# Expert gating with its counts ahead of its ranks, and one wait of the key-shared attention placed behind a projection

## The reference

```python
probs = jax.nn.softmax(x @ gate_w, axis=-1)
w, sel = jax.lax.top_k(probs, K)                    # K = 8 of E = 32
w = w / jnp.sum(w, axis=-1, keepdims=True)
flat_e = sel.reshape(-1)
order = jnp.argsort(flat_e)
se = flat_e[order]
start = jnp.searchsorted(se, jnp.arange(E))
pos = jnp.arange(P) - start[se]
slot = jnp.where(pos < C, se * C + pos, E * C)      # C = 2 * (P // E)
```

```python
gating = jax.nn.softmax(x @ W_gate.T, axis=-1)
idx = jnp.argmax(gating, axis=-1)
indicator = jax.nn.one_hot(idx, H, dtype=gating.dtype)
gating_top1 = indicator * jnp.max(gating, axis=-1, keepdims=True)
q, k, v = jnp.split(x @ W_qkv.T, 3, axis=-1)
k_shared = jnp.einsum('bth,bthd->btd', indicator, k)
v_shared = jnp.einsum('bth,bthd->btd', gating_top1, v)
att = softmax(causal(einsum('bhqd,bkd->bhqk', q, k_shared) / sqrt(hd)))
y = jnp.einsum('bhqk,bkd->bhqd', att, v_shared)
```

## Time and profile before

| what | value |
|---|---|
| median of three runs | 2397.06 us |
| profiled execution, its own time | 2396.05 us |
| its span | 2394.0 us |
| PE busy | 2161.7 us (90%) |
| PEld busy | 1379.3 us (58%) |
| DVE busy | 1525.1 us (64%) |
| ACT busy | 1116.3 us (47%) |
| POOL busy | 741.6 us (31%) |
| mean granted TensorE clock | 0.958 |

### The profile page before, as it was taken

One profiled execution on the slowest core, in us unless ns is written; L12 is line 12 of the kernel. 1 busy time (PEld: TensorE's weight loads), 2 busy tenths in 40 slices (PEclk: granted clock), 3 DMA queues, 4 the chain that ended last, 5 costly groups with the idle time before them and its releaser, 6 DMA issues. The chain is left out here.

```text
span 2394.0 us, 38433 instructions
## 1 busy us (share of the span) xinstructions
PE 2161.7 (90%) x10486; PEld 1379.3 (58%) x10486; DVE 1525.1 (64%) x3718; ACT 1116.3 (47%) x3541; POOL 741.6 (31%) x930
## 2 busy tenths in 40 slices
PE   6978999989799799979999999999998698879999
PEld 3445677766555344445565666566665455545675
DVE  6975434446566577755577777777777688842234
ACT  2021234421355355545555655565554488822342
POOL 5715510046233200013344444444443200003104
PEclk9968999999999899989999999999999699969999
DMA  6902245544400000000000000000000000201243
GB/s 214 312 29 77 91 125 161 164 153 115 170 1 0 3 1 0 0 27 1 1 1 1 0 1 0 1 1 0 1 0 1 5 6 5 109 3 52 68 130 100
DMA packets 85614, 127.41 MB, mean 53 GB/s; under 512 B 12418, under 2 KB 74626, under 8 KB 84226
## 3 DMA queue, kind: packets, MB, share of 16 engines
q1 hardware_dynamic: 75490, 98.52, 12.8%
q0 software_dynamic: 9984, 27.28, 3.6%
HBM read 91.41 MB, written 47.84 MB: 58 GB/s over the span
## 5 line engine op out<-in xcount | busy, mean ns | idle before, releaser
L2442 ACT ACTIVATE l2x_prob<-l2x_pS,l2x_nb,l2x_rms_q 128x256 f32<-128x256 f32 x256 | 142.5, 565 | 147.1 <-DVE l2x_nb L2691 145.3
L1035 ACT ACTIVATE moe_act_g<-moe_pG 128x96 f32<-128x96 f32 (+1 forms) x159 | 53.4, 336 | 266.2 <-PE moe_pU L968 185.8
L1199 PE MATMUL l2x_pQ<-big,l2x_xT 128*128 128x512 f32 x312 | 149.6, 602 | 4.8 <-DVE l2x_part L2669 4.3
L3212 DVE TENSOR_TENSOR l3f_hid<-l3f_act_g,l3f_pA 128x256 f32<-128x256 f32 (+1 forms) x103 | 38.1, 370 | 163.3 <-ACT l3f_act_g L3123 119.5
L928 POOL DMA_INDIRECT moe_yk<-route_y,moe_slot_i x72 | 71.4, 992 | 216.2 <-DMA route_y<-moe_y 187.6
L2240 PE MATMUL l2x_pOT<-l2x_probT,l2x_v 128*128 128x512 f32 x256 | 126.4, 616 | 12.3 <-ACT l2x_probT L2457 12.3
L2230 PE MATMUL l2x_pS<-l2x_kT,l2x_qT 128*128 128x256 f32 x512 | 129.8, 383 | 0.0
L3036 PE MATMUL l3f_pA<-big,l3f_xnT 128*128 128x512 f32 x256 | 126.1, 617 | 0.0
L2247 PE MATMUL l2x_pT<-big,l2x_oT 128*128 128x256 f32 x512 | 123.8, 379 | 0.0
L3123 ACT ACTIVATE l3f_act_g<-l3f_pA 128x256 f32<-128x256 f32 (+1 forms) x103 | 35.4, 344 | 184.6 <-PE l3f_pA L3036 184.6
L2688 DVE TENSOR_REDUCE l2x_negmax<-l2x_pS 128x2 f32<-128x512 f32 x128 | 87.5, 684 | 52.3 <-PE l2x_pS L2230 50.6
(11 more groups left out here) (538 smaller groups left out, 5735.8 us busy)
## 6 DMA issues: line engine op xcount, KB each, us to landing
route_x<-in_c_zero SPq DMA_DIRECT2D x1, 13184.0 KB, 80.5
moe_xg<-route_x SPq DMA_DIRECT2D x103, 128.0 KB, 2.1
route_y<-moe_y SPq DMA_DIRECT2D x103, 128.0 KB, 1.7
big<-in_e_gu SPq DMA_DIRECT2D x1, 6144.0 KB, 18.9
l3f_xg<-route_x SPq DMA_DIRECT2D x39, 128.0 KB, 2.2
route_y<-l3f_y SPq DMA_DIRECT2D x39, 128.0 KB, 1.7
big<-in_f_gu SPq DMA_DIRECT2D x1, 4096.0 KB, 12.5
big<-in_e_down SPq DMA_DIRECT2D x1, 3072.0 KB, 25.6
```

What stands on the lines that cost most here:

```text
L1199: last = pe.matmul(out, lhsT=xT[:, k, :], rhs=w[:, k, cols], start=(k == 0), stop=(k == KC - 1))
L2442: ins = act.activation(prob[g % 2][:, h, :], pS[j][:, (h % 2) * 2 * P:(h % 2 + 1) * 2 * P], ACT.Exp, scale=rms_q[g][:, h:h + 1], bias=nb[: ...
```

## The change

In gating the nine matmuls of the counts go ahead of those of the ranks and raise a semaphore of their own, `counts`. VectorE rounds the counts behind that one. The triangle `below`, its load and the product with it are gone; the offsets come from a running sum over the 32 experts in five rounds, each a copy of the first columns and an addition of the rest shifted by 1, 2, 4, 8 or 16. `until` is the scaled sum and `offs` that minus the expert's own count. The weights are normalised next, and only then does VectorE wait for `ranks` and make the slots. In the key-shared attention the wait for `normalised` moves from ahead of the value projection to behind it, ahead of the projection into `pQK`.

```diff
@@ -696,10 +696,10 @@
         replaced, top = ph.sb("replaced", [P, B, NE]), ph.sb("top", [P, B, 8])
         chosen, probs = ph.sb("chosen", [P, B, NE], BF16), ph.sb("probs", [P, B, NE])
         red, rec = ph.sb("red", [P, B]), ph.sb("rec", [P, B])
-        lower, onesb, below = ph.sb("lower", [P, P], BF16), ph.sb("onesb", [P, P], BF16), ph.sb("below", [P, NE * NE])
-        prod = ph.sb("prod", [P, NE, NE])
-        const_in, xT_ps, xT_ready, logits, steps, masks, ranks, exp_done = (
-            ph.sem(n) for n in ("const_in", "xT_ps", "xT_ready", "logits", "steps", "masks", "ranks", "exp_done"))
+        lower, onesb = ph.sb("lower", [P, P], BF16), ph.sb("onesb", [P, P], BF16)
+        sums = [ph.sb(f"sums{i}", [P, NE]) for i in range(2)]
+        const_in, xT_ps, xT_ready, logits, steps, masks, counts, ranks, exp_done = (
+            ph.sem(n) for n in ("const_in", "xT_ps", "xT_ready", "logits", "steps", "masks", "counts", "ranks", "exp_done"))
         need, offs, until, slot = G["need"], G["offs"], G["until"], G["slot"]
         block = ph.block()
 
@@ -720,7 +720,6 @@
         def _(sp):
             sp.dma_start(lower[:].bitcast(U16), D["c_lower"]).then_inc(const_in, 16)
             sp.dma_start(onesb[:].bitcast(U16), D["c_onesb"]).then_inc(const_in, 16)
-            sp.dma_start(below[:], D["c_below32"].partition_broadcast(P)).then_inc(const_in, 16)
 
         @block.tensor
         def _(pe):
@@ -747,15 +746,16 @@
                 turn(b)
                 scores(b - 1)
             scores(B - 1)
-            pe.wait_ge(const_in, 48)
+            pe.wait_ge(const_in, 32)
             pe.wait_ge(masks, 1)
             picked = chosen[:].rearrange("p b e -> p (b e)")
+            for b in range(SB):
+                last = pe.matmul(pC[:, 0:NE], lhsT=onesb[:], rhs=chosen[:, b, :], start=(b == 0), stop=(b == SB - 1))
+            last.then_inc(counts, 1)
             pe.matmul(pR[:], lhsT=lower[:], rhs=picked, start=True, stop=True)
             for d in range(1, B):
-                pe.matmul(pR[:, d * NE:], lhsT=onesb[:], rhs=picked[:, 0:(B - d) * NE], start=False, stop=True,
-                          skip_group_check=True)
-            for b in range(SB):
-                last = pe.matmul(pC[:, 0:NE], lhsT=onesb[:], rhs=chosen[:, b, :], start=(b == 0), stop=(b == SB - 1))
+                last = pe.matmul(pR[:, d * NE:], lhsT=onesb[:], rhs=picked[:, 0:(B - d) * NE], start=False, stop=True,
+                                 skip_group_check=True)
             last.then_inc(ranks, 1)
 
         @block.scalar
@@ -771,7 +771,7 @@
 
         @block.vector
         def _(dve):
-            ch = Chain(dve, steps, 2 * B + 13)
+            ch = Chain(dve, steps, 2 * B + 15)
             ch.turn(0)
 
             def best(b):
@@ -796,23 +796,28 @@
                 L = pL[t][:, 0:B // 2 * NE].rearrange("p (b e) -> p b e", e=NE)
                 ch(dve.tensor_tensor(probs[:, t::2, :], L, top[:, t::2, 0:1].to_broadcast([P, B // 2, NE]),
                                      ALU.subtract))
-            dve.wait_ge(masks, 1)
-            dve.wait_ge(ranks, 1)
+            dve.wait_ge(counts, 1)
             ch(dve.tensor_scalar(need[:], pC[:, 0:NE], 1.0 / P, 63.5 / P, ALU.mult, ALU.add))
             ch(dve.tensor_scalar(need[:], need[:], ROUND, -ROUND, ALU.add, ALU.add))
-            ch(dve.tensor_tensor(prod[:], need[:].unsqueeze(1).to_broadcast([P, NE, NE]),
-                                 below[:].rearrange("p (e f) -> p e f", e=NE), ALU.mult))
-            ch(dve.tensor_reduce(offs[:], prod[:], AX.X, ALU.add))
+            src = need
+            for i in range(5):
+                dst, n = sums[i % 2], 1 << i
+                dve.tensor_copy(dst[:, 0:n], src[:, 0:n])
+                ch(dve.tensor_tensor(dst[:, n:NE], src[:, n:NE], src[:, 0:NE - n], ALU.add))
+                src = dst
+            ch(dve.tensor_scalar(until[:], src[:], float(P), None, ALU.mult))
+            ch(dve.scalar_tensor_tensor(offs[:], need[:], -float(P), until[:], ALU.mult, ALU.add))
+            dve.wait_ge(exp_done, 1)
+            dve.wait_ge(masks, 1)
+            ch(dve.tensor_tensor(probs[:], probs[:], chosen[:], ALU.mult))
+            ch(dve.tensor_reduce(red[:], probs[:], AX.X, ALU.add))
+            ch(dve.reciprocal(rec[:], red[:]))
+            ch(dve.tensor_tensor(probs[:], probs[:], bc(rec[:], NE), ALU.mult))
+            dve.wait_ge(ranks, 1)
             R = pR[:].rearrange("p (b e) -> p b e", e=NE)
             ch(dve.scalar_tensor_tensor(slot[:], R[:, 0:SB, :], 1.0, offs[:].unsqueeze(1).to_broadcast([P, SB, NE]),
                                         ALU.add, ALU.add))
             ch(dve.tensor_tensor(slot[:], slot[:], chosen[:, 0:SB, :], ALU.mult))
-            ch(dve.scalar_tensor_tensor(until[:], need[:], float(P), offs[:], ALU.mult, ALU.add))
-            dve.wait_ge(exp_done, 1)
-            ch(dve.tensor_tensor(probs[:], probs[:], chosen[:], ALU.mult))
-            ch(dve.tensor_reduce(red[:], probs[:], AX.X, ALU.add))
-            ch(dve.reciprocal(rec[:], red[:]))
-            ch(dve.tensor_tensor(probs[:], probs[:], bc(rec[:], NE), ALU.mult))
             dve.scalar_tensor_tensor(G["w_all"][:], R, float(CAP), probs[:], ALU.is_lt, ALU.mult)
 
 
@@ -1654,8 +1659,8 @@
             def qkv(b, p):
                 pe.wait_ge(nm.xT_ready, b + 1)
                 after(pe, qkv_read, b)
+                project(pe, pV[:, 0:C + NH], nm.xT[p], W["W_vg"]).then_inc(qkv_ps, 1)
                 after(pe, sm.normalised, b - 2)
-                project(pe, pV[:, 0:C + NH], nm.xT[p], W["W_vg"]).then_inc(qkv_ps, 1)
                 project(pe, pQK[:], nm.xT[p], W["W_qk"]).then_inc(qkv_ps, 1)
                 if isinstance(b, int) and b == 0:
                     ternary.spread(pe)
```

## The result

| | before | after |
|---|---|---|
| median of 5 runs | 2397.06 us (2395.65 to 2403.93) | 2387.14 us (2382.38 to 2390.42) |
| profiled execution, its own time | 2396.05 us | 2386.48 us |
| its span | 2394.0 us | 2384.3 us |
| mean granted TensorE clock | 0.958 | 0.958 |

After takes 0.9958 of before, 95% interval 0.9944 to 0.9971: 9.9 us less at the medians, where 9.0 were forecast. I cut both spans at the first instruction of each phase. Gating went from 38.9 to 34.8 us, the key-shared attention from 239.4 to 235.1, all other phases together changed by -1.4: -4.1 - 4.3 - 1.4 = -9.8, the 9.7 us between the spans but for rounding.

A forecast was written before the change was run, and what follows sets the result against it. VectorE was taken to set gating's end, and a VectorE-TensorE ring of 13.97 us the attention's turn. Gating -3.8 (-3.01 - 2.73 + 1.94) and attention -5.2 make -9.0: 2388.1 us; own range 2386 to 2390, 8 in 10 2385 to 2393.

The forecast's parts named there:

- The counts' wait: End of gating: with the counts' matmuls first, VectorE's wait of 3.19 us shrinks to 0.18, 3.01 us less.
- The cheap end: Counts' term in gating: VectorE starts `need` at once, at 172.65 us, giving -3.16 instead of -3.01.
- The running sum: Offsets in gating: 1.94 us of new copies, additions and small instructions replace 2.73 us of removed ones.
- the row: Trace row of a VectorE copy: it delayed the next instruction by 0.09 us though it lasted 0.18.
- The cover: Gating: exponentials (173.28, wanted 175.2) and ranks (about 176.4, slots wanted 177.7) finish before VectorE needs them, costing nothing.
- The clock at the experts' start: Start of the experts' phase: TensorE still starts at 0.50 near 180.0 us; effect taken as 0.
- Rival 3: Experts' phase starts at the full clock, 2.4 us more saved: 2385.7 us; chance 0.09.
- rival 4: Experts' phase fails to get the full clock, 4.2 us more per item, 2409 us with five; chance 0.03.
- The attention: Key-shared attention: the moved wait wins the whole wait for `att`, 0.40 us a turn, 13 times, 5.2 us.
- the best end: Attention's upper limit: overlap of matmuls with no wait between adds 0.16 us a turn, 7.3 us in 13.
- Rival 1: The attention gives nothing to the end, as VectorE is busy most of the turn: 2393.3 us; chance 0.09.
- Rival 2: Gating's counts come late and its small instructions cost much: -1.1, with half the attention's gain 2393.4 us; chance 0.07.

The follow-up runs named there:

- counts_again: counts_only run once more: before with the counts' nine matmuls ahead of the ranks, old way to the offsets, attention unmoved; 2394.07 us in one run, gating 36.1 us.
- again: The changed kernel (after), unchanged, run once more against before: 2387.24 us against 2395.58, ratio 0.9957.
- gate_only: After with the attention's wait where it was in before, so only gating is changed: 2388.93 us, ratio 0.9970 to before.
- attn_only: Before with only the attention's wait moved behind the value projection: 2392.17 us, ratio 0.9989 to before.
- attn_again: attn_only once more on another chip (before with only the attention's wait moved): 2393.89 us, ratio 0.9988 to before.
- padded: After with the running sum's tiles widened by 16 zero columns, so the five copies fall away: 2386.23 us, ratio 0.9955 to before.
- pool_mask: After with the product of exponentials and chosen mask on GpSimd instead of VectorE: 2379.24 us in one run, gating 35.1 us.
- best: After with zero-padded sum tiles, GpSimd masking the exponentials and VectorE's `att` ahead of `ternary`: 2409.74 us on the slower chip, ratio 0.9960 to before.
- counts_only: Before with the counts' matmuls first and their own semaphore, the rest as before: 3640.71 us at a granted clock of 0.555, gating 36.2 us.
- scan_only: Before with the running sum in place of the triangle, the rest as before: 2411.41 us in one run on the slower chip (before 2418.08).
- div_after: After with VectorE's `att` put ahead of the filler work of `ternary`: 2409.23 us where before took 2418.08, ratio 0.9963.

## Why the prediction was right

**The counts' wait**, forecast -3.01, measured -3.17 (4.07 to 0.90 from `probs` to `need`). I took the nine matmuls as doubled, 0.76 us, since the clock stood at 0.50. They took 0.40, against 0.38. The cheap end of that term was the true one: `need` waits for nothing. The marks in absolute time came 0.3 us late, `need` at 173.11 for 172.8 and the experts' first matmul at 180.29 for 180.0, as gating itself began 0.5 us later in this trace (145.5 for 145.0).

**The running sum**, forecast 1.94 us in and 2.73 out. Measured 175.44 - 173.55 = 1.89 in. A round is 173.84 - 173.55 = 0.29, forecast 0.30. An addition starts 0.07 to 0.08 us behind its copy though the copy lasts 0.15 to 0.17: the row carried, and the copy didn't cost its whole duration. The Trainium skill ("VectorE: DVE Perf Modes", section "The DRAIN you can't avoid") has the rule that the prediction set against it, but adds in the same section that a next operation that is not held starts earlier; the prediction left that out, and the trace agrees with it. The time from `need` to `w_all` went from 6.65 to 178.88 - 173.11 = 5.77 us: -0.88 for -0.79.

**The cover.** Exponentials done at 173.74, wanted at 175.44; ranks done at 176.26 (forecast 176.4), slots at 177.90 (forecast 177.7). counts_again shows that the reordering was worth 0.40 and not nothing: without it the ranks come late.

**The clock at the experts' start**, taken as 0. First before, its clock around the rise and the fourth group of matmuls, then after:

```profile
188.00:190.00 2.00, 2.00 (x7) 1.17 (x6) 0.39 (x1) 0.49 (x1) 0.03 (x1) 0.84 0.00 0
```

```profile
190.17 1.45 PE L968 MATMUL moe_pU<-big,moe_data_xnT 128*128 128x384 f32 x4
```

```profile
179.00:186.00 7.00, 5.71 (x9) 3.17 (x10) 1.71 (x12) 1.49 (x2) 0.00 (x0) 0.52 0.25 56
186.00:188.00 2.00, 2.00 (x7) 1.14 (x6) 1.11 (x2) 0.28 (x1) 1.21 (x1) 0.97 0.00 0
```

```profile
187.14 1.45 PE L973 MATMUL moe_pU<-big,moe_data_xnT 128*128 128x384 f32 x4
```

TensorE starts at 180.29 at the lower level and has the full clock from 186.1 (0.97 over two us is 0.12 us at 0.50), 5.8 us on. In before it came at 188.6, 4.8 us on. Its first twelve matmuls took 187.14 - 180.29 = 6.85 us instead of 190.17 - 183.86 = 6.31. So one of the prediction's own signs of being wrong came true, a clock of 0.50 beyond five us, at a price of 0.5 us and not of whole items. It differs from trace to trace: the same stretch is 6.52 us in again, 6.78 in gate_only, 6.21 and 6.28 in attn_only and attn_again, and 5.34 in padded, which had the full clock 2.8 us on. Rival 3 came out in none of them in full, rival 4 only in that small size; the term is +0.2 to +0.5 us in the changed kernel's two traces and not 0.

**The attention.** Forecast 0.40 us a turn. The middle shows (166.8 - 160.7) / 12 = 0.51. Of this the moved wait gave 0.44, as attn_only and attn_again show with 161.5 us each, and that is the term but for 0.04: the overlap that I had kept for the best end is there in part, as `pV` starts at 937.71, 0.06 before `pO` ends at 937.77. The other 0.07 a turn is the shorter wait for the shared key, which came with the gating edit. The middle makes about 6 us, inside the forecast's own range. In after's trace 2.8 us of it are hidden by the lower clock at the phase's start, which gate_only shows without the moved wait, and which attn_only and attn_again show to come and go with one and the same program.

**Rival 1** falls by attn_only's turn, and by its time at equal clock; the plain ratio alone (2.5 us won) would have spoken half for it. **Rival 2** falls by gating's 34.8 us. The forecast sum, -9.0, came out as -9.9; the parts at equal clock are -4.0 and -5.4, which sum to -9.4, and together they measured -10.3 +- 1.7. As plain differences of means they are -6.5 and -3.7, together -10.1 measured.

That the whole came so near is in part luck. The forecast's two terms are there in the trace, -4.1 and -5.3. But so are terms that it had not: +2.8 at the attention's start, -1.0 at its end, -0.8 by the shared key, +0.5 at the experts' start, and -1.3 in a stretch of layer 2's phase (772.5 us instead of 773.8). The last is there in gate_only (772.1) and counts_again (772.4) too and not in attn_only (774.0) or attn_again (773.9), so it goes with the gating edit (pool_mask, with 773.2, lies between), in code that the edit doesn't touch. No run tells why.

## What to carry to other kernels

A wait on one semaphore that covers two results prices the early one like the late one: give the short result its own and put it first, then check that what the other one feeds has moved behind enough work. If a wait guards only the second of two matmul groups, put it between them, and read the turn length rather than the whole time to see it work. Before work goes from VectorE to GpSimd, look at what VectorE runs beside it: in both kernels that put two-tensor instructions on SBUF side by side, VectorE's stood still.

## What the runs showed of the hardware

- A two-tensor instruction of VectorE, all in SBUF, stood still during one of GpSimd: 1.065 and 1.169 us instead of 0.19 and 0.18, in both kernels that had the two side by side. The Trainium skill ("SBUF — State Buffer", section "SBUF: two separate sides") has this as an exclusive lock that whoever comes first holds for the whole instruction. The two traces agree for GpSimd first, 0.14 and 0.03 us ahead of the long addition; VectorE first isn't shown here. I had not looked for it when best was written.
- The smallest matmuls here hardly felt the clock: nine of 32 columns took 0.40 us at 0.50 and 0.38 at 1.00, while of the experts' matmuls with 384 columns eight took 5.02 us, nearly all of it at 0.50, and four took 190.17 - 188.88 = 1.29 at 1.00.
- Executions of the same program differ in their mean clock, by 0.006 among the twelve runs of attn_only, and with each 0.001 the time went by 1.5 to 1.9 us. A difference of 5 us needed a dozen runs and the clock beside them. The one execution of counts_only had 0.555, from end to end of its trace; one of before in the first group had the same mean (3644.79 us) and is left out of the fit.
- The experts' phase took longer on one chip: 447.9 to 451.7 us in the three traces taken there at the usual clock (scan_only, best, div_after), against 426.3 to 432.9 in the ten from elsewhere. There is no trace of before from that chip; its median is 21 to 22.5 us above those on the others. The other phases moved by what they vary from one execution to the next. Why, no run here tells.
